# Query norm moved from the exponential into the masking pass, gate operands in PSUM, and a new instruction order, in a one-core transformer layer

## The reference

```
x = x + attention(layernorm(x));   x = x + ffn(layernorm(x))
attention: q = x wq.T (16 heads of 64), k, v (4 heads of 64, each for 4 q heads)
  q = q * rsqrt(mean(q*q) + eps) * q_norm_w;   k likewise
  scores = q k.T / 8, only keys j with i - 127 <= j <= i;  y = softmax(scores) v;  y wo.T
ffn: gate = softmax(x gate_w.T) over 8 experts
  out = x weight.T + (1/16) * sum over experts of gate[e] * lora_V[e] (lora_U[e] x)
```

## Time and profile before

| | |
|---|---|
| median of 3 runs | 2243.64 us (2242.95 to 2248.56) |
| the profiled execution: its time | 2248.26 us |
| its span | 2246.4 us |
| mean granted TensorE clock | 0.991 of full speed |
| busy share PE, DVE, ACT, POOL | 94%, 94%, 89%, 51% |

### The profile page before, as it was taken

How to read it: one execution, slowest core, us unless ns; L and a number is a source line. 1 busy time by engine, 2 the same in 40 slices (tenths; PEclk the granted TensorE clock), 3 DMA queues, 4 the chain that set the end, 5 groups by cost and what they waited for, 6 DMA issues and landing times.

```text
span 2246.4 us, 109187 instructions
## 1 busy us (share of the span) xinstructions
PE 2108.1 (94%) x42768; PEld 1678.6 (75%) x42768; DVE 2103.2 (94%) x8998; ACT 1995.4 (89%) x6663; POOL 1152.4 (51%) x1036
## 2 busy tenths in 40 slices
PE   7999999999999999999999999999999999999997
PEld 5777777777777777777777777777777777777775
DVE  7999999999999999999999999999999999999996
ACT  7899988998898899989988899899888998998895
POOL 3555555555455545555554455545554555555452
PEclk9999999999999999999999999999999999999998
DMA  3111111111111111111111111111111111111110
GB/s 105 46 49 53 48 48 47 51 48 48 48 51 48 49 52 46 49 47 52 49 48 47 49 47 49 48 52 47 48 48 48 51 49 46 52 48 49 48 40 23
DMA packets 138206, 110.95 MB, mean 49 GB/s; under 512 B 37216, under 2 KB 136928, under 8 KB 137696
## 3 DMA queue, kind: packets, MB, share of 16 engines
q1 hardware_dynamic: 137696, 103.97, 17.0%
HBM read 19.93 MB, written 16.78 MB: 16 GB/s over the span
## 4 chain that ended last, share of the span: by engine, by line
PE 37%; DVE 35%; issue 14%; ACT 13%; DVEq 0%; DMA 0%; POOL 0%; SPq 0%
PE ps_y L740 10%; DVE soft L495 10%; DVE pT L522 5%; PE ps_scores L724 5%; PE ps_y L678 4%; DVE yT_l L528 4%; ACT soft L347 4%; ACT yT_h L363 3%; DVE q_ms L478 3%; PE ps_e L672 2%; PE ps_e L674 2%; PE ps_e L673 2%; PE ps_y L672 2%; PE ps_y L674 2%; PE ps_y L673 2%
## 5 line engine op out<-in xcount | busy, mean ns | idle before, releaser
L347 ACT ACTIVATE soft<-soft,neg_max,q_r 128x160 f32<-128x160 f32 x2048 | 1043.4, 516 | 25.6 <-DVE neg_max L505 24.6
L272 POOL TENSOR_TENSOR soft<-soft,rden 128x640 f32<-128x640 f32 x384 | 481.0, 1253 | 793.1 <-DVE rden L511 793.1
L522 DVE STREAM_TRANSPOSE pT<-soft 128x640 f32<-128x640 f32 x512 | 424.0, 828 | 57.3 <-PE ps_y L740 53.6
L724 PE MATMUL ps_scores<-kT,qT 64*32 64x160 f32 (+4 forms) x16384 | 392.3, 286 | 46.8 <-issue 26.9
L261 POOL TENSOR_TENSOR q_r<-q_ve,minus_half 128x8 f32<-128x8 f32 x256 | 420.5, 1642 | 2.5 <-DVE q_ve L485 2.5
L495 DVE CUSTOM_DVE_ANT_0 soft<-ps_scores,mask_band 128x160 f32<-128x160 f32 x1536 | 400.9, 316 | 0.5 <-issue 0.2
L347 ACT ACTIVATION_READ_ACCUMULATOR soft<-soft,neg_max,q_r 128x1 f32 x2048 | 398.1, 194 | 0.0
L740 PE MATMUL ps_y<-pT,v_rep 32*64 32x128 f32 x17920 | 324.8, 276 | 50.9 <-issue 46.8
L740 PEld LDWEIGHTS ps_y<-pT,v_rep 32*64 32x64 f32 x17920 | 285.3, 131 | 87.8 <-issue 58.0
L724 PEld LDWEIGHTS ps_scores<-kT,qT 64*32 64x32 f32 x16384 | 227.9, 106 | 164.2 <-issue 108.0
L672 PE MATMUL ps_e<-wo_h,yT_h 128*128 128x256 f32 x1024 | 305.7, 299 | 5.5 <-issue 1.8
(11 more groups left out here) (105 smaller groups left out, 4719.3 us busy)
## 6 DMA issues: line engine op xcount, KB each, us to landing
v_rep<-v_own SPq DMA_DIRECT2D x2048, 32.0 KB, 1.9
xs<-x SPq DMA_DIRECT2D x128, 128.0 KB, 2.3
out<-ob SPq DMA_DIRECT2D x128, 128.0 KB, 2.1
w_plain<-w_qkv SPq DMA_DIRECT2D x3, 512.0 KB, 4.7
w_plain<-w_o SPq DMA_DIRECT2D x8, 128.0 KB, 5.4
w_plain<-w_ffn SPq DMA_DIRECT2D x1, 392.0 KB, 5.9
w_plain<-w_v SPq DMA_DIRECT2D x1, 128.0 KB, 5.1
nw<-norm_w SPq DMA_DIRECT2D x1, 1.0 KB, 5.2
```

Of the source, the lines that this page charges most:

```text
L272: pool.tensor_tensor(soft[:, r], soft[:, r], rden[:, r].unsqueeze(2).to_broadcast([P, REP, SPAN]), ALU.mult).then_inc(s_pn, 1)
L347: last = nc.scalar.activation(soft[:, r, h], soft[:, r, h], ACT.Exp, bias=neg_max[:, r, h:h + 1], scale=q_r[:, T % DEEP, head:head + 1], a ...
L522: nc.vector.transpose(pT[:, g // 2, :, g % 2].rearrange("p e c k -> p e (c k)"), soft[:, ring(T, g)].rearrange("p (e c) k -> p e (c k)", e ...
L724: last = nc.tensor.matmul(ps_scores[queries, 2 * half + c, first - begin:SPAN], qT[rows, T % 2, 2 * g + c, queries], kT[rows, g // 2, at + ...
```

## The change

The query norm moves. The masking pass takes q_r as the scale of the scores, so soft holds normed scores. All signs are turned: qk_w is negative, the mask is +1e30, the pass takes the minimum, and this minimum is the bias of the exponential, whose scale is the constant -1. `scaled_max` and its semaphore s_max are gone; `mask_and_max` now waits for `q_power`, and `exps` waits for the masking pass itself.

The gate's g_neg and g_exp lie in unused columns of the PSUM bank of ps_ffn instead of SBUF.

The banks are dealt anew: q's first half to a, its transposes to b and c, k, v, kT and hT to f, ps_o to d, ps_ffn to e. The steps of all four computing engines have another order, and some operations move by a whole step (TensorE's loop has one more step, ScalarE's begins one earlier).

```diff
-        ps_q = [ps_e, ps_c]
-        ps_qT = [ps_b, ps_b]
-        ps_kv, ps_kT, ps_xT, ps_hT, ps_tT = ps_d, ps_a, ps_a, ps_d, ps_a
-        ps_o, ps_ffn = ps_e, ps_f
+        ps_q = [ps_a, ps_c]
+        ps_qT = [ps_b, ps_c]
+        ps_kv, ps_kT, ps_xT, ps_hT, ps_tT = ps_f, ps_f, ps_a, ps_f, ps_a
+        ps_o, ps_ffn = ps_d, ps_e
+        g_neg, g_exp = ps_ffn[:, FFN_OUT:FFN_OUT + 1], ps_ffn[:, FFN_OUT + EXPERTS:FFN_OUT + 2 * EXPERTS]
...
-                    act.wait_ge(s_max, groups(T, g))
+                    act.wait_ge(s_mm, groups(T, g))
...
-                        last = nc.scalar.activation(soft[:, r, h], soft[:, r, h], ACT.Exp, bias=neg_max[:, r, h:h + 1], scale=q_r[:, T % DEEP, head:head + 1],
-                                                    accum_out=den[:, r, h:h + 1])
+                        last = nc.scalar.activation(soft[:, r, h], soft[:, r, h], ACT.Exp, bias=neg_max[:, r, h:h + 1], scale=-1.0, accum_out=den[:, r, h:h + 1])
...
+                    dve.wait_ge(s_s, groups(T, g))
+                    dve.wait_ge(s_qr[g // 2], done(T))
                     wait(dve, s_pt, groups(T, g) - RING)
-                    dve.wait_ge(s_s, groups(T, g))
...
-                        last = nc.vector.tensor_tensor_reduce(soft[:, r, h], ps_scores[:, h, 0:SPAN], mask_band[:] if slot(T) else mask_first[:], 1.0, LOWEST,
-                                                              ALU.add, ALU.max, accum_out=raw_max[:, r, h:h + 1])
+                        last = nc.vector.tensor_tensor_reduce(soft[:, r, h], ps_scores[:, h, 0:SPAN], mask_band[:] if slot(T) else mask_first[:],
+                                                              q_r[:, T % DEEP, head:head + 1], HIGHEST, ALU.add, ALU.min, accum_out=neg_max[:, r, h:h + 1])
```

More of the change, by code:

```diff
@@ L26 @@
 LN_EPS, RMS_EPS = 1e-5, 1e-6
-MASKED, LOWEST = -1e30, -3e38
+MASKED, HIGHEST = 1e30, 3e38
 CONSTANTS = 8
@@ L373, in gate_exp @@
                     act.wait_ge(s_gmax, done(T))
-                    nc.scalar.activation(g_exp[:, T % DEEP], ps_ffn[:, DIM + ER:FFN_OUT], ACT.Exp, bias=g_negmax[:, T % DEEP], scale=h_rstd[:, T % DEEP], accum_out=g_den[:, T % DEEP]).then_inc(s_gexp, 1)
+                    nc.scalar.activation(g_exp, ps_ffn[:, DIM + ER:FFN_OUT], ACT.Exp, bias=g_negmax[:, T % DEEP], scale=h_rstd[:, T % DEEP], accum_out=g_den[:, T % DEEP]).then_inc(s_gexp, 1)
             def high_tg(T):
@@ L381, in step @@
             def step(T):
[L382 to L392, removed]
+                square_q(T + 2, 0)
+                exps(T, 0, range(0, 2))
+                high_tg(T - 3)
                 store_v(T + 1)
-                high_x(T + 2)
-                exps(T - 1, 3, range(2, 4))
-                exps(T, 0, range(0, 2))
                 exps(T, 0, range(2, 4))
@@ L399, in step @@
                     high_weights(W_FFN)
-                high_tg(T - 3)
+                square_q(T + 2, 1)
+                copy_q(T + 2, 1)
+                high_x(T + 3)
                 store_qT(T + 1, 0)
-                normalise(T - 1, 3)
                 high_h(T - 2)
-                copy_q(T + 1, 1)
-                square_q(T + 1, 1)
+                exps(T, 1, range(0, 2))
+                exps(T, 1, range(2, 4))
+                high_y(T - 1, 0)
+                high_y(T - 1, 1)
                 store_kT(T + 1)
-                copy_q(T + 2, 0)
-                square_q(T + 2, 0)
-                exps(T, 1, range(0, 2))
+                exps(T, 2, range(0, 2))
+                exps(T, 2, range(2, 4))
+                exps(T, 3, range(0, 2))
+                gate_exp(T - 2)
+                exps(T, 3, range(2, 4))
+                square_k(T + 2)
+                store_qT(T + 1, 1)
+                if T == -1:
+                    high_weights(W_O, W_V)
+                normalise(T, 3)
+                copy_q(T + 3, 0)
             high_x(0, early=True)
             high_weights(0, 1, 2)
-            for T in range(-2, TILES + 3):
+            for T in range(-3, TILES + 3):
                 step(T)
@@ L592, in step @@
             def step(T):
+                sum_q(T, 1)
+                k_mean_square(T)
+                gate_t(T - 4)
+                transpose_probs(T - 2, 2)
+                transpose_probs(T - 2, 3)
                 x_mean_and_var(T + 1)
[L594 to L597, removed]
                 mask_and_max(T - 1, 1)
@@ L601, in step @@
                     low_o_weights(2)
+                q_mean_square(T - 1, 1)
+                low_tg(T - 4)
+                norm_k(T)
+                sum_q(T + 1, 0)
+                add_x(T - 3)
+                inverse(T - 1, 0)
                 h_statistics(T - 3)
[L603 to L606, removed]
+                low_x(T + 2)
                 h_mean_and_var(T - 3)
-                sum_q(T, 0)
+                q_mean_square(T, 0)
                 mask_and_max(T - 1, 2)
@@ L623, in step @@
                     low_lora_weights()
+                low_y(T - 2, 0)
+                low_y(T - 2, 1)
+                gate_max(T - 3)
+                inverse(T - 1, 2)
                 gate_max_normed(T - 3)
-                scaled_max(T - 1, 3)
-                sum_q(T, 1)
+                transpose_probs(T - 1, 1)
                 x_statistics(T + 2)
-                inverse(T - 1, 2)
-                transpose_probs(T - 1, 1)
-                gate_inverse(T - 3)
-                gate_share(T - 3)
                 mask_and_max(T, 0)
@@ L790, in step @@
             def step(T):
+                if live(T + 1):
+                    freed(pe, (s_yl, T - 3, pairs(T - 3, 1)), (s_xtl, T + 1, done(T + 1)))
+                    project_q(T + 1, 0)
+                if live(T - 3):
+                    project_out(T - 3, 1)
+                if live(T - 3):
+                    project_out(T - 3, 2)
+                if live(T - 1):
+                    freed(pe, (s_mm, T - 1, groups(T - 1, 0)))
+                    scores(T - 1, 1)
+                if live(T - 4):
+                    freed(pe, (s_qsq[0], T + 1, done(T + 1)), (s_yl, T - 3, pairs(T - 3, 1)), (s_xtl, T + 1, done(T + 1)), (s_ttl, T - 5, done(T - 5)))
+                    transpose_tg(T - 4)
+                if live(T + 1):
+                    freed(pe, (s_qT[1], T - 1, done(T - 1)), (s_yl, T - 3, pairs(T - 3, 1)), (s_qc[1], T, done(T)))
+                    project_q(T + 1, 1)
+                if live(T - 3):
+                    project_out(T - 3, 3)
+                if live(T + 2):
+                    freed(pe, (s_ttl, T - 4, done(T - 4)), (s_qsq[0], T + 1, done(T + 1)), (s_yl, T - 3, pairs(T - 3, 1)), (s_xtl, T + 1, done(T + 1)))
+                    transpose_x(T + 2)
+                if live(T):
+                    freed(pe, (s_yl, T - 3, pairs(T - 3, 1)), (s_qT[0], T - 1, done(T - 1)))
+                    transpose_q(T, 0)
+                if live(T - 4):
+                    add_lora(T - 4)
+                if live(T - 3):
+                    freed(pe, (s_kn, T, done(T)), (s_kT, T - 1, done(T - 1)), (s_htl, T - 4, done(T - 4)))
+                    transpose_h(T - 3)
                 if live(T - 1):
```

120 lines of the change are left out of this document (38 added, 82 removed).

## The result

The changed kernel takes 2228.44 us (median of 8 runs, 2224.58 to 2235.74) against 2244.4 for the kernel before in as many runs: ratio 0.9934, 95% interval 0.9914 to 0.9954. It is faster, by 0.7% where 2.8% was forecast: 2228 lies inside the stated range of 2110 to 2265, but three quarters of the gain are missing. The profiled execution has a span of 2226.6 us; 2180 was the sum.

The account below looks back on a forecast made before the run. VectorE at 16.3 us per step plus TensorE stalls in long attends bounds the kernel. Short steps 15.6, long 16.0 + 1.0, mean 16.65 against 17.22: 70 us less, about 4 added, so 2180 us; range 2110 to 2265.

Parts of the forecast that it names:

- the parts' prices: Per tile: VectorE loses 2.28 us and gains 1.5 for the masking passes' scalar; ScalarE's exponentials lose 1.5.
- Rival 1: VectorE's masking pass, reading mask and q_r from SBUF, is held by POOL: 1.5 to 3 us per tile, 2300 to 2430; chance 0.08.
- Rival 2: ScalarE becomes the bound: exponentials stay at 516 ns while new waits stay, 17.3 us per step, 2250 to 2290; chance 0.08.
- POOL ... is no bound: POOL keeps its five kinds of operation, 9.0 us per tile, and does not set a step.
- the sum of VectorE's step, 15.5 us: VectorE's work per tile: 14.0 us after the removals plus 1.5 for the masking passes' scalar.
- The dense stretch: TensorE's scores 2, attend, scores 3: 32 + 160 + 32 products, as long as before, so 1.0 us of stalls per long step stays.
- the stalls of the old order: TensorE's stalls in the kernel before: about 89 us, 0.93 per long step, on top of VectorE's 16.3.
- the start: One more, nearly empty step, placed at the end, costs about 4 us.
- Rival 3: VectorE's gain goes into TensorE's stalls, growing from 1.0 to 1.7 per long step: 2240 to 2250 us; chance 0.07.

Follow-up runs that it names:

- old_order_both: Kernel before with both parts of the change (gate operands in PSUM, norm in the masking pass), old order and old banks: 2185.8 us, ratio 0.9731.
- new_order_early_qms: Changed kernel with VectorE's q_mean_square(T, 0) moved in front of q_mean_square(T-1, 1): 2213.92 us, ratio 0.9853 to the kernel before.
- The split: new_order_early_qms with scores 2 moved in front of add_lora and transpose_h, and transpose_k in front of scores 3: 2187.51 us, ratio 0.9754.
- late copies: Copies of v for tile T + 1 start behind attend(T-1) instead of attend(T-2); on old_order_both 2174.73 us (0.971), on new_order_early_qms 2200.26 us (0.9825).

## Why the prediction was wrong

**Right: the parts' prices.** The gate's operations (1.0 us per tile less forecast; 933 and 463 ns became 156 and 158), ScalarE's exponential (0.102 forecast, 0.097 measured), the pass's scalar between its bounds (0 to 0.095; 0.062, so 1.0 us per tile where 1.5 was taken). Rival 1 fell: a masking pass (L498) runs beside POOL's division in 124 of 128 steps, and its mean is 378 ns with no pass over 389. Rival 2 fell with the exponential. The time of 2180 is near what the two parts give in the old order, 2185.8, with short steps of 15.62 and long ones of 17.1 where 15.6 and 17.0 were forecast. What failed is what I said of the new order.

**Wrong: "POOL ... is no bound" and the sum of VectorE's step, 15.5 us.** I moved the gate and the scaled maximum out of the collision and didn't ask which other operation with two SBUF inputs the new order would put there. VectorE's step is 14.0 + 16 x 0.062 + (1.04 - 0.16) = 15.9, and 15.92 is what the median short step takes. That my sum came within 0.4 of it is luck: the scalar taken 0.5 too dear hid half of the missing 0.88. Shown by the moved line: 15.53 us, 18 us in all.

**Wrong: "The dense stretch ... is as long as before, so the stalls stay".** They grew, from 74 us idle to 105, and the long steps are 17.35 where I had 17.0. The step that failed is the inference from the length of the stretch to the length of the stalls. A stall is TensorE at the edge of a 16 KB packet of instructions that hasn't landed 1.2 us before, so it takes a number of fast matmuls in front of the edge, and these may stand in front of scores 2 as well. In old_order_both no attend stalls before 117 of its matmuls are through. In new_order_early_qms the stalls begin after 73, and with add_lora and transpose_h behind scores 2, but for two of them, after 111 again. With half the attend's products nothing stalls. The split takes back 22 us of the 27 that new_order_early_qms stands behind old_order_both, and the rest is within the intervals. Which neighbour does most of it wasn't tried alone.

**Right: the stalls of the old order.** I took 0.93 us per long step from the idle time. The attends cut short gave back 92 us on 96 steps in the old order, 0.96. So the size was right there. But 16.3 + 0.93 is 17.2 and the long steps of before took 17.53: the account of them lacked 0.3 us from the start.

**Mis-sized: the start.** The first L590 of before starts at 81.1 us, L584 at 88.2 after and at 79.4 in old_order_both. The new order costs 9 us at the start, where I had 4 for its added step at the end. The split has 84.0, so part of the 9 is where the operations stand and not the added step.

Rival 3 (stalls grow from 1.0 to 1.7) comes closest to what happened: the stalls grew by about half as much as it has, and the collision makes up for much of the rest. I held against it that the short steps never stall. That says what the stalls need (the long attend), not that they stay as they are.

Left open: why the norm's move alone loses 0.12 us in the long steps, why the gate alone gives only 0.36 there, and whether the late copies help at all (3 comparisons, 4 to 6 us each, none clear of its interval).

## What to carry to other kernels

When an operation leaves a collision, list every operation of the same kind and see which one the new order puts there; a row that is clean before (156 ns) says only that its neighbour was idle. Price a new order by trying the change's contents in the old one: here the contents gave 2.7 points and the order took 2.0 of them away. And where a chain of some hundred tiny matmuls stalls for "issue", count the matmuls from stall to stall and compare with the packets of the instruction queue. If they agree, put long matmuls between the chain's parts: project_ffn between the attend and scores 3 gave 27 us, while add_lora's three in front of the attend gave nothing.

## What the runs showed of the hardware

- A VectorE operation with two SBUF tensors waits for POOL's running tensor operation (1.04 us for 0.16); the same operation with one of the two in PSUM doesn't (156 ns), and neither does a pass with a PSUM tensor, an SBUF tensor and a per-partition scalar of SBUF (378 ns).
- A per-partition scalar costs the VectorE pass 0.062 us, and ScalarE's activation 0.097.
- TensorE's instructions arrive in DMA packets of 16 KB, here 125 matmuls with their loads (342 packets for 42768 matmuls). A stall at such an edge ended 1.2 to 1.6 us behind the packet's landing, 931 times of 931.
- TensorE, in 224 matmuls with a load each, lost 0.96 us on average where 144 lost nothing. Cutting the DMA queue's data from 104 to 39 MB took 3 us of 69 us of idle time away.
